# Start of a fused attention and channel-mix kernel: statistics ahead of norms, one norm on ScalarE, fold and second queries between score blocks, weight planes later

## The reference

```python
# attention: mixed precision over the contraction dimension
y1 = jnp.matmul(x[..., :K_LOW1].astype(jnp.float16), w1.astype(jnp.float16)).astype(jnp.float32)
yh = jnp.matmul(x[..., K_LOW1:d - K_LOW2], wh)
y2 = jnp.matmul(x[..., d - K_LOW2:].astype(jnp.float16), w2.astype(jnp.float16)).astype(jnp.float32)
...
qk = jnp.einsum('bqd,bkd->bqk', q, k)
s = jax.nn.softmax(qk, axis=-1)
y = jnp.einsum('bqk,bkd->bqd', s, v)
return jnp.matmul(y, out_w.T) + out_b
...
# channel mix
xr = mu_r * x + (1.0 - mu_r) * x_prev
xk = mu_k * x + (1.0 - mu_k) * x_prev
r = jax.nn.sigmoid(jnp.einsum('btc,dc->btd', xr, W_r))
k_act = jnp.square(jax.nn.relu(jnp.einsum('btc,dc->btd', xk, W_k)))
out = r * jnp.einsum('btc,dc->btd', k_act, W_v)
...
x = x + _layernorm(attn(_layernorm(x)))
x = x + _layernorm(ffn(_layernorm(x)))
```

## Time and profile before

| | |
|---|---|
| median of 3 runs | 814.92 us (814.14 to 815.58) |
| the profiled execution | 815.95 us, its span 814.2 us |
| busy, share of the span | TensorE 784.2 us (96%), VectorE 655.9 (81%), ScalarE 574.8 (71%), GpSimd 512.9 (63%) |
| mean granted TensorE clock | 0.991 |
| chain that ended last | TensorE 90%, VectorE 4%, DMA 2% |

### The profile page before, as it was taken

One profiled execution on the slowest core, in us unless ns is written; L12 is line 12 of the kernel. 1 busy time (PEld: TensorE's weight loads), 2 busy tenths in 40 slices (PEclk: granted clock), 3 DMA queues, 4 the chain that ended last, 5 costly groups with the idle time before them and its releaser, 6 DMA issues.

```text
span 814.2 us, 16555 instructions
## 1 busy us (share of the span) xinstructions
PE 784.2 (96%) x5835; PEld 574.4 (71%) x5835; DVE 655.9 (81%) x1685; ACT 574.8 (71%) x791; POOL 512.9 (63%) x750
## 2 busy tenths in 40 slices
PE   7889999999999999999999999999999999998983
PEld 5446677777777777777777777777777777777872
DVE  6688788777888879887878879887777788778876
ACT  3486658876778778787678687877776776775564
POOL 2250346567577758866756776876567567576674
PEclk9999999999999999999999999999999999999998
DMA  6377789687667779767567986857677655569301
GB/s 203 76 155 144 153 154 169 114 162 143 137 122 143 145 143 188 143 116 142 101 138 147 188 162 136 147 100 136 120 143 143 130 117 89 122 120 201 81 14 52
DMA packets 348243, 108.70 MB, mean 134 GB/s; under 512 B 321920, under 2 KB 347904, under 8 KB 348160
## 3 DMA queue, kind: packets, MB, share of 16 engines
q1 hardware_dynamic: 348160, 107.64, 68.2%
HBM read 18.75 MB, written 8.39 MB: 33 GB/s over the span
## 4 chain that ended last, share of the span: by engine, by line
PE 90%; DVE 4%; DMA 2%; issue 1%; ACT 1%; POOL 1%; SPq 0%; POOLq 0%; DVEq 0%; ACTq 0%
PE Y L1475 7%; PE Y L1479 7%; PE Y L1477 7%; PE Y L1478 7%; PE Y L1476 7%; PE S L1454 6%; PE S L1458 6%; PE S L1455 6%; PE S L1457 6%; PE S L1456 6%; PE M L1419 6%; PE M L1421 6%; PE M L1420 6%; PE M L1434 1%; PE M L1435 1%
## 5 line engine op out<-in xcount | busy, mean ns | idle before, releaser
L1131 DVE TENSOR_SCALAR_CACHE_REDUCE probs<-S 128x512 f32<-128x512 f32 x256 | 172.8, 676 | 65.4 <-PE S L1458 65.3
L1149 DVE TENSOR_TENSOR p_lo<-probs,p_hi 128x2048 f16<-128x2048 f32 x62 | 170.0, 2742 | 7.3 <-ACT p_hi L750 7.1
L818 ACT ACTIVATE probs<-probs,exp_bias,kappa 128x2048 f32<-128x2048 f32 x64 | 133.9, 2092 | 58.7 <-DVE exp_bias L1144 58.7
L1475 PE MATMUL Y<-pt_hi,planes 128*128 128x256 f16 x496 | 135.2, 273 | 0.0
L1477 PE MATMUL Y<-pt_hi,planes 128*128 128x256 f16 x496 | 135.2, 273 | 0.0
L1478 PE MATMUL Y<-pt_lo,planes 128*128 128x256 f16 x496 | 135.2, 273 | 0.0
L1476 PE MATMUL Y<-pt_lo,planes 128*128 128x256 f16 x496 | 135.2, 273 | 0.0
L1479 PE MATMUL Y<-pt_hi,planes 128*128 128x256 f16 x496 | 135.2, 273 | 0.0
L750 ACT ACTIVATE p_hi<-probs 128x2048 f16<-128x2048 f32 x64 | 121.4, 1897 | 7.1 <-DMA pt_lo<-p_lo 7.0
L1454 PE MATMUL S<-turned,q_hi 128*128 128x512 f16 x256 | 97.3, 380 | 9.4 <-DVE q_lo L1122 5.9
L1456 PE MATMUL S<-turned,q_hi 128*128 128x512 f16 x256 | 97.3, 380 | 0.0
(11 more groups left out here) (223 smaller groups left out, 2033.4 us busy)
## 6 DMA issues: line engine op xcount, KB each, us to landing
x_res<-in_L_attn_x SPq DMA_DIRECT2D x32, 256.0 KB, 3.7
out_x<-gate SPq DMA_DIRECT2D x32, 256.0 KB, 3.4
xs<-in_L_attn_x SPq DMA_DIRECT2D x13, 512.0 KB, 4.6
pt_hi<-p_hi SPq DMA_TRANSPOSE x62, 5.0
pt_lo<-p_lo SPq DMA_TRANSPOSE x62, 4.8
xs<-in_L_attn_x SPq DMA_DIRECT2D x2, 256.0 KB, 4.0
gate<-in_L_attn_x SPq DMA_DIRECT2D x1, 512.0 KB, 7.9
att<-in_L_attn_x SPq DMA_DIRECT2D x1, 512.0 KB, 4.4
```

The costliest lines, as they stand in the source:

```text
L1131: dve.tensor_scalar(probs[:, h % 2, t, c * BLK:(c + 1) * BLK], S[k % RING][:, :], 1.0, None, ALU.mult, ALU.max, accum_out=chunk_max[:, t, ...
L1149: dve.tensor_tensor(p_lo[:, t, :], probs[:, h % 2, t, :], p_hi[:, t, :], ALU.subtract).then_inc(p_lo_made, 1)
L1475: pe.matmul(to[:, 0, :], low, p_h, start=first, stop=False, skip_group_check=True)
```

## The change

- On VectorE the first statistics tile of block 1 is taken ahead of `weight_scale()` and a second one ahead of `weight_factors()`; the statistics and moments of blocks 1, 2 and 3 all come before the first block norm.
- The norm of block 1 goes from VectorE to ScalarE (`pre_norm(1)` there, with `pminus` and `pshift` on GpSimd and a semaphore of its own, `pre_normed_act`). Block 2's norm stands ahead of slot 0 on VectorE, block 3's in slot 0. On GpSimd `pre_rsqrt(3)` now stands ahead of `planes_low(1)`.
- `queries(1)` and the fold go between slots 1 and 2 on TensorE (from slots 2 and 3), `query_high(1)` and `row_norms_of()` ahead of slot 0 on ScalarE. The transposes of the last three weights go from slot 5 to slot 7, their peaks from slot 4 to 1.
- Turning, spreading and topping the peaks moves from slots 11, 12, 15, 16 to 15, 17, 19, 20; the high planes from slots 17 and 19 to 24 and 27, the low planes from 18 and 20 to 25 and 28.
- `query_low(h)` stands ahead of `probs_low` within a slot.
- The filler matmuls are 22, 8, 28, 16 instead of 22, 18, 18, 12.
- On SP the four loads of `mu` stand ahead of the transpose of block 1, and the rows of the first two blocks of the second sequence are loaded right after the start list instead of in slots 15 and 26.

```diff
-    NORMS_AT = (0, 1)
+    NORM_AT = 0
     V_AT = 1
-    WEIGHT_PEAKS_AT = 4
+    WEIGHT_PEAKS_AT = 1
     FIRST_LOW = 2
-    WARM = (22, 18, 18, 12)
+    WARM = (22, 8, 28, 16)
...
-    FOLD_AT, WEIGHTS_AT, VAL_AT, PEAKS_AT, PEAKS_TURN_AT, DIAGONAL_AT, SPREAD_AT, TOPS_AT = 3, 5, 6, 8, 11, 12, 15, 16
-    W_HIGH_AT, W_LOW_AT = (17, 19), (18, 20)
+    WEIGHTS_AT, VAL_AT, PEAKS_AT, PEAKS_TURN_AT, DIAGONAL_AT, SPREAD_AT, TOPS_AT = 7, 9, 8, 15, 17, 19, 20
+    W_HIGH_AT, W_LOW_AT = (24, 27), (25, 28)
...
# SP
-            turn_planes(1)
             for i, m in enumerate((mu_r, mu_k)):
...
+            turn_planes(1)
             turn_planes(2)
             turn_planes(3)
...
+            reload_x(NJ)
+            reload_x(NJ + 1)
...
# GpSimd, pre_rsqrt(n) and the start list
+                if n == 3:
+                    pool.wait_ge(pre_normed_act, NT)
...
             pre_rsqrt(2)
+            pre_rsqrt(3)
             planes_low(1)
-            pre_rsqrt(3)
             planes_low(2)
...
# ScalarE
             query_high(0)
+            pre_norm(1)
             planes_high(1)
...
             planes_high(3)
+            query_high(1)
+            row_norms_of()
...
# VectorE
             half_norm(0)
+            dve.wait_ge(x_in[1], 16)
+            stats_of(1, range(1))
             weight_scale()
             half_low(0)
             half_norm(1)
+            stats_of(1, range(1, 2))
             weight_factors()
             half_low(1)
-            dve.wait_ge(x_in[1], 16)
-            stats_of(1, half(0))
+            stats_of(1, half(1))
             qk_low()
-            stats_of(1, half(1))
             pre_moments_of(1)
             pre_stats_of(2)
-            pre_norm(1)
+            pre_moments_of(2)
             query_low(0)
-            pre_moments_of(2)
             pre_stats_of(3)
+            dve.wait_ge(pre_shift_made, 1)
+            pre_moments_of(3)
+            pre_norm(2)
...
# TensorE
-                if (h := at(k, QUERY)) is not None and h >= 1:
-                    pe.wait_ge(q_lo_made, h)
-                    queries(h)
                 if k == V_AT:
                     pe.wait_ge(w_rounded, 2)
                     turn_weight(2)
                     turn_weight(3)
-                if k == FOLD_AT:
+                    pe.wait_ge(q_lo_made, 1)
+                    queries(1)
                     multiply_weights(2, 3, FOLD_BANK, out_multiplied)
+                if (h := at(k, QUERY)) is not None and h >= 2:
+                    pe.wait_ge(q_lo_made, h)
+                    queries(h)
```

More of the change, by code:

```diff
@@ L285, in sandwich @@
         pre_stats = sem("pre_stats"); pre_moments = sem("pre_moments"); pre_eps = sem("pre_eps")
-        pre_rstd = sem("pre_rstd"); pre_normed = sem("pre_normed")
+        pre_rstd = sem("pre_rstd"); pre_normed = sem("pre_normed"); pre_normed_act = sem("pre_normed_act")
         half_in = sem("half_in"); half_eps = sem("half_eps"); half_rstd = sem("half_rstd"); half_hi_made = sem("half_hi_made")
@@ L351, in low_made, with by_act, act_norms @@
             return p_lo_made, h * RT + t + 1 - min(h + 1 if t == 1 else h, FIRST_LOW)
+        def by_act(n):
+            return n == 1 or n >= NJ
+        def act_norms(n):
+            return 1 if n < NJ else n - NJ + 2
         def rows_of(n):
@@ L458, in _ @@
                     turn_planes(n)
-                if (n := prep(k, PREP_LOAD)) is not None:
+                if (n := prep(k, PREP_LOAD)) is not None and n >= NJ + 2:
                     reload_x(n)
@@ L516, in pre_rsqrt @@
                 pool.tensor_tensor(prstd[:, i, :], pvar[:, i, :], minus_half[:, :], ALU.pow).then_inc(pre_rstd, 1)
-                if n >= NJ:
-                    pool.wait_ge(pre_turned, n - NJ + 1)
+                if by_act(n):
+                    pool.wait_ge(pre_turned, act_norms(n))
                     pool.wait_ge(pre_rstd, n)
@@ L783, in pre_norm @@
                 i = n % 2
-                act.wait_ge(pre_shift_made, n - NJ + 1)
+                act.wait_ge(pre_shift_made, act_norms(n))
                 for t in range(NT):
@@ L787, in pre_norm @@
                     act.activation(o, o, ACT.Identity, bias=pshift[:, i, t:t + 1],
-                                   scale=prstd[:, i, t:t + 1]).then_inc(pre_normed, 1)
+                                   scale=prstd[:, i, t:t + 1]).then_inc(pre_normed_act, 1)
             def copy_high(n, tiles, done):
@@ L804, in planes_high @@
                     act.wait_ge(pv_done, (b - 1) * PER)
-                act.wait_ge(pre_normed, (n + 1) * NT)
+                if by_act(n):
+                    act.wait_ge(pre_normed_act, act_norms(n) * NT)
+                else:
+                    act.wait_ge(pre_normed, n * NT)
                 copy_high(n, slice(0, NT), plane_hi_made)
@@ L936, in _ @@
                         split_high(h, i)
-                if (h := at(k, Q_HIGH)) is not None and h >= 1:
+                if (h := at(k, Q_HIGH)) is not None and h >= 2:
                     query_high(h)
@@ L945, in _ @@
                 if k == VAL_AT:
-                    row_norms_of()
                     keep_val()
@@ L1304, in _ @@
                 score_out(k)
-                if k == NORMS_AT[0]:
-                    pre_norm(2)
-                    pre_moments_of(3)
-                if k == NORMS_AT[1]:
+                if k == NORM_AT:
                     pre_norm(3)
@@ L1313, in _ @@
                     gated(h)
+                if (h := at(k, Q_LOW)) is not None and h >= 1:
+                    query_low(h)
                 if (ht := exp_at(k, FIRST_LOWER, LOWER)) is not None and (ht[1] > 0 or ht[0] >= FIRST_LOW):
@@ L1325, in _ @@
                         mix(h, i)
-                if (h := at(k, Q_LOW)) is not None and h >= 1:
-                    query_low(h)
                 if (h := at(k, INVERT)) is not None:
```

4 lines of the change are left out of this document (2 added, 2 removed).

## The result

The changed kernel takes 809.12 us (median of 4 runs, 807.10 to 809.71), the kernel before 814.76 us beside it (4 runs): a ratio of 0.9926, 95% interval 0.9906 to 0.9945, 5.6 us less. The forecast was 808.9. The profiled execution took 809.13 us.

A forecast was written before the change was run, and what follows sets the result against it. TensorE, full from 100 to 700 us, was taken as the bound, leaving only the start to gain. 3.1 + 1.2 + 1.5 = 5.8, rounded to 6.0, off a median of 814.92 gave 808.9 us; range 806.8 to 811.6.

The forecast's parts named there:

- The bound: TensorE is full from 100 to 700 us and the drain is unchanged, so what is gained at slot 24 is kept.
- Part 1: VectorE's start: block 1's statistics wait for its rows until 10.6, w_peak begins 1.0 us late, queries(0) end 0.93 late.
- Part 2: Block 1's norm on ScalarE: q_lo(0) follows q_hi directly, slot 0 begins at 18.0 against 18.84, planes_low(1) 0.6 us late.
- the fillers set slot 0: TensorE's start: the sixteen filler matmuls end at 18.0, so slot 0 begins then.
- planes_low(1) would start 0.6 late behind block 3: GpSimd: pre_rsqrt(3), now ahead, waits for block 3 until 21.0 or 21.1; the transpose lands near 26.15.
- Part 3: Gap ahead of slot 2: queries(1) and fold take 2.82 us off the path, half clock's 1.31 us gone; 3.5 net.
- Part 4: Slot 6: block 3's norm meets GpSimd's planes_low, its transposed planes come late; 0.4 us charged, 3.1 us left.
- The stall of 0.4 at slot 6: Block 3's transpose lands at 30.7 to 30.9, while slot 6 could start at 30.5; 0.4 us charged.
- Parts 5 and 6: Slots 16 to 24: q_lo(2) ahead of p_lo nets 1.2 us; low weight planes moved to slots 25 and 28 net 1.5.
- The wait at slot 17: Slot 17 needs slot 14's score copy, now behind p_lo on VectorE; 0.75 us late, charged against the 1.95 gained.
- the one of weight_scale_of for GpSimd: Slot 20 on VectorE: weight_scale_of waits for GpSimd's p_lo(1,0), making q_lo(3) 0.7 us late for slot 24; bounds 0 and 0.7.
- cover: Slots 24 to 32: TensorE needs 18.5 us, VectorE some 17.4, so slot 32 finds q_lo(4) about 1.1 us early.

The follow-up runs named there:

- e7_stats: The changed kernel with the four statistics tiles of block 1 back in their old places; 808.17 us, ratio 0.9911 to the kernel before.
- e8_tops: The changed kernel with only the tops moved from slot 20 to 21, behind q_lo(3); 808.0 us, ratio 0.9906 to the kernel before.
- e5_filler: The kernel before with 28 filler matmuls added between slot 1's weight transposes and slot 2; 818.2 us, ratio 1.0027.
- e3_planes: The kernel before with only the peaks, tops and weight planes moved to slots 15, 17, 19, 20 and 24 to 28; 812.56 us, ratio 0.9955.
- e2_qlow: The kernel before with only query_low put ahead of probs_low in its slot; 815.26 us, ratio 0.9993.
- e1_front: The changed kernel with query_low behind probs_low again and the weight tables in their old slots; 812.61 us, ratio 0.9948 to the kernel before.
- c_before: The kernel before, unchanged, profiled a second time; 816.32 us in one execution.
- c_after: The changed kernel, unchanged, measured once more; 808.74 us, ratio 0.9909 to the kernel before.

## Why the prediction was right

The size was right, 5.8 rounded to 6.0 against 5.6. The mechanism was right in the main: work moved into the gap ahead of slot 2, and VectorE's chain to the low queries of slot 24 shortened. The working has one wrong price and one wrong kind of sum, and its errors partly cancel.

- **The bound.** Right: 100 to 700 us stayed full, and from slot 24 to the last slot all profiles took 670.2 us, but for 1.7 us more in the two whose clock fell behind slot 24. In 11 of 14 profiles what follows slot 24 took 751.2 to 751.7 us; the other three are e7_stats, e8_tops and e5_filler. The drain is not as fixed as the prediction took it, see the last section.
- **Part 1** failed. "It sits until 10.6": in the changed kernel the rows of block 1 landed 5.9 us after issue, not 7.0 as in the earlier trace rows, and 5.2 to 6.6 in all later profiles (at most 6.3 with the new start list); I took one execution's landing for a constant. w_peak started 2.03 us behind the product of weights, just as before (10.19 - 8.16, 9.93 - 7.90), and 2.03 to 2.07 behind it in all 14 profiles. The tile (0.42 us) fills the 0.41 us that VectorE idled ahead of w_peak in the earlier trace rows, an idle piece that the prediction left out. It cost nothing, and its price of about 0.9 us on the start was not paid. What a landing of 7.0 us would cost the changed kernel, no run shows.
- **Part 2.** q_lo(0) no longer waits for the norm: right. That the fillers set slot 0: wrong, it waited for the transpose of half block 1, 0.53 and 2.02 us in two profiles. Slot 0 at 17.99, forecast 18.0, was luck: the second profile has it at 19.78. From the product of weights, slot 0 comes after 10.9 us in every profile with the start list of before, and after 9.83 and 11.32 us in the two of the changed kernel. That planes_low(1) would start 0.6 late behind block 3: wrong with Part 1; relative to the product of weights it starts 0.1 to 0.2 earlier.
- **Part 3** held: 2 to 6 fell by 5.44 = 2.82 of moved work + 1.31 of weight transposes moved on + 1.31 of clock. The clock fell behind this gap in both profiles of before, but not in e3_planes, where the wait was as long (3.26 us). In e2_qlow it fell behind slot 0 instead, and in the second profile of the changed kernel too, where that cost 1.3 us. So the 1.31 us is a gain of this pair of profiles and not of every one.
- **Part 4.** The norm of block 3 met GpSimd and took 1.94 instead of 1.38: right. The stall of 0.4 at slot 6 did not come. At slot 6 the gain was 35.31 - 29.91 - 1.31 = 4.1, not 3.1: slot 2 came at 25.59 and not at 26.15, and the stall was missing. In the second pair of profiles it was 2.8.
- **Parts 5 and 6** together: -2.7 forecast; measured 6 to 16 down by 2.25 (without the moved transposes) and 16 to 24 by 0.50, -2.75. Their split was wrong: q_lo alone gained nothing from slot 6 to slot 24 (e2_qlow), since the chain behind it is as long as before, and the tables alone were worth 2.5 by stages. The wait at slot 17 was 1.02 by issue, not 0.75; the one of weight_scale_of for GpSimd cost 0.31, not 0.7, the rest hidden behind 0.3 us that the spreading matmul of slot 19 added to TensorE. Slots 24 to 32 had cover, as said: 18.47 us.
- By the Trainium skill (SBUF — State Buffer, "Who interferes with whom") a VectorE instruction in a two-port mode and a GpSimd one exclude each other, and the one that issues later is blocked for the whole of the other. The runs agree: weight_scale_of ended at 54.53 where GpSimd's p_lo ended at 54.50, at 57.79 against 57.76 and at 55.46 against 55.43, and it took 0.17 us where GpSimd was done. Which mode it ran in, the profile doesn't show.
- The terms missed by +1.0 at the front and the first pair of profiles shows 6.84 us at slot 24; the medians of the first set show 5.6, those of the last 6.9. Single executions of either kernel differ by 2 to 5 us, in the landing of the first rows and weights (the product of weights starts between 7.86 and 8.55) and in where the clock falls. So the agreement of 808.9 with 809.12 is closer than the working deserved.

## What to carry to other kernels

An operation put ahead of another on a busy engine moves a wait; it removes one only if the engine's chain to the next deadline is shortened or begins earlier, so add such edits along the chain and not one by one. Filling a gap pays only as far as the filling is ready in time: of some 4.1 us (2.82 of work and 1.31 of clock) the fold alone kept 2.6 from the product of weights to slot 6, the changed kernel 4.4 in its first profile and 3.2 in its second, beside the profiles of before. Before pricing a new wait for a transfer, take its landing from several executions. A fall of the clock was free only where TensorE still waited behind it.

## What the runs showed of the hardware that I had not expected

The granted clock fell to 0.50, the lower of its two levels (1.2 GHz), for 3 to 4 us behind waits of only 1.8 to 2.1 us (slot 16 in e1_front, slot 24 in e5_filler and c_before, slot 0 in e2_qlow and c_after), and in other profiles it stayed at 1.00 behind the same waits, once even behind 3.26 us (e3_planes). A fall costs up to 1.7 us where TensorE has no wait to spare (24 to 32 took 20.15 us instead of 18.46 in c_before), 1.3 us in c_after, and nothing where a long enough wait follows: in e2_qlow the wait ahead of slot 2 shrank to 1.82 us and slot 2 came 6.70 us behind slot 0, as before.

The drain has such a place too. From the last slot's scores to the end it took 81.0 to 81.4 us in ten profiles in which the clock fell near 740 us, and 79.4 to 79.6 us in the three in which it did not (e7_stats, e8_tops, c_before); e5_filler, with its longer wait, took 82.9. Busy times near 740 us in c_after and in e8_tops:

```profile
741.00:742.00 1.00, 1.00 (x7) 0.69 (x6) 1.00 (x1) 0.00 (x0) 0.99 (x1) 0.50 1.25 166
```

```profile
740.00:741.00 1.00, 1.00 (x12) 0.90 (x10) 1.00 (x1) 0.00 (x0) 1.00 (x1) 1.00 1.00 161
```

So the equal 751.4 and 751.3 us behind slot 24 in c_before and c_after are a coincidence: the one lost 1.7 us behind slot 24, the other in the drain.

A mean granted clock is known for every run. Of the 52 runs of the kernel before beside the experiments, the 8 with a mean of 0.990 or less took 817.4 us on average, the 7 with 0.996 took 814.2, and the 37 between them 815.8. The changed kernel's five runs of c_after had 0.994 to 0.998. So part of the spread of the kernel before (812.97 to 818.21 us) goes with how long the clock is down, and part of the gain may too; how much of the 5.6 us it is in an average run stays open.
